# Four instead of seven buffers for the scatter rows and weights of the routed tiles (cross attention and a top-2 mixture of experts on one core)

## What is computed

```python
x = x + xattn(layernorm(x), ctx)                 # 16 heads, causal
scores = sigmoid(xf @ gate_w + bias)
top_scores, top_idx = top_k(scores, 2)           # normalised to sum 1
up = einsum('th,ehi->tei', xf, up_w) + up_b
eo = einsum('tei,eih->teh', gelu(up), down_w) + down_b
combined = einsum('teh,te->th', eo * 0.1, w)     # the two chosen experts
shared = (gelu(xf @ sw_up + sb_up) @ sw_down + sb_down) * 0.1
out = shared + combined;  out = out / (max|out| + 1e-6)
x = x + out
```

## Time and profile before

| | us |
|---|---|
| median of three runs | 898.97 |
| the three runs | 898.99, 898.97, 893.63 |
| the profiled execution | 898.99 |
| its span, first to last instruction | 897.3 |
| around the span (898.99 - 897.3) | 1.7 |
| mean granted PE clock of the span, share of 2.4 GHz | 0.963 |
| busy over the span: PE; DVE; ACT; POOL | 810.9 (90%); 650.1 (72%); 652.1 (73%); 556.1 (62%) |

### The profile page before, as it was taken

How to read it: one execution, slowest core, us unless ns; L and a number is a source line. 1 busy time by engine, 2 the same in 40 slices (tenths; PEclk the granted TensorE clock), 3 DMA queues, 4 the chain that set the end, 5 groups by cost and what they waited for, 6 DMA issues and landing times.

```text
span 897.3 us, 21771 instructions
## 1 busy us (share of the span) xinstructions
PE 810.9 (90%) x7005; PEld 549.7 (61%) x7005; DVE 650.1 (72%) x1767; ACT 652.1 (73%) x1185; POOL 556.1 (62%) x647
## 2 busy tenths in 40 slices
PE   3899999989999999999887639999999999999994
PEld 1355555545555555554455527888888888888773
DVE  6665668777677787765664446878787878777797
ACT  3478897877877877876695628988888888889630
POOL 7267565877878787876565733065656565667531
PEclk9999999989999999998898868999999999999998
DMA  4533543441222222211001124576777787891983
GB/s 118 163 119 106 190 138 107 124 153 55 69 68 74 74 59 85 79 47 48 26 23 54 52 72 153 194 265 233 267 235 264 240 284 274 296 291 63 235 241 105
DMA packets 101382, 128.84 MB, mean 144 GB/s; under 512 B 21143, under 2 KB 81367, under 8 KB 95255
## 3 DMA queue, kind: packets, MB, share of 16 engines
q1 hardware_dynamic: 92183, 108.04, 37.9%
q0 software_dynamic: 9088, 19.42, 6.1%
HBM read 78.79 MB, written 40.56 MB: 133 GB/s over the span
## 4 chain that ended last, share of the span: by engine, by line
PE 60%; issue 11%; DVE 10%; ACT 9%; POOL 8%; another core or an unknown queue 1%; SPq 0%; DMA 0%; ACTq 0%; DVEq 0%; POOLq 0%
PE bank L1291 8%; PE bank L1276 6%; ACT prob L734 5%; POOL y_scratch L1157 5%; PE bank L1373 4%; PE bank L1371 4%; PE bank L1382 4%; PE bank L1384 4%; PE bank L1383 4%; PE bank L1372 4%; PE bank L1296 3%; PE bank L1308 3%; PE bank L1269 3%; PE bank L1251 2%; PE bank L1256 2%
## 5 line engine op out<-in xcount | busy, mean ns | idle before, releaser
L734 ACT ACTIVATE prob<-bank,padb,sc 120x512 f32<-120x512 f32 x256 | 178.3, 777 | 80.0 <-PE bank L1296 72.0
L1157 POOL DMA_INDIRECT y_scratch<-yo,ti x156 | 156.7, 1004 | 123.3 <-DVE yo L1067 86.8
L1135 POOL TENSOR_SCALAR_AFFINE_SELECT prob<-prob 120x512 f32<-120x512 f32 x256 | 162.3, 637 | 86.7 <-ACT prob L734 81.5
L804 DVE TENSOR_REDUCE nm<-bank 128x4 f32<-128x480 f32 x256 | 150.4, 650 | 68.2 <-PE bank L1276 68.2
L1046 DVE TENSOR_TENSOR gl<-gf,gh 128x512 fp32r<-128x512 f32 x220 | 153.3, 699 | 56.0 <-ACT gh L780 49.5
L1150 POOL DMA_INDIRECT xs_scratch<-x2r,idx x128 | 126.9, 992 | 49.6 <-issue 32.9
L780 ACT ACTIVATE gh<-gf 128x512 fp32r<-128x512 f32 x220 | 138.5, 629 | 5.1
L1291 PE MATMUL bank<-qblk,kT 32*120 32x512 f32 x512 | 116.3, 652 | 0.1
L775 ACT ACTIVATE gf<-bank,wt 128x512 f32<-128x512 f32 x156 | 105.9, 679 | 0.2
L775 ACT ACTIVATE gf<-bank,shb 128x512 f32<-128x512 f32 x64 | 43.6, 682 | 49.4 <-remote 17.6
L1276 PE MATMUL bank<-kblk,qT 32*128 32x480 f32 x512 | 72.5, 633 | 0.0
(11 more groups left out here) (194 smaller groups left out, 1663.5 us busy)
## 6 DMA issues: line engine op xcount, KB each, us to landing
wt<-w_scratch SPq DMA_DIRECT2D x39, 1032.0 KB
xt<-xs_scratch SPq DMA_DIRECT2D x39, 280.0 KB
w_scratch<-x2t SPq DMA_DIRECT2D x8, 1024.0 KB, 5.2
wt<-y_scratch SPq DMA_DIRECT2D x28, 256.0 KB, 5.0
xs_scratch<-padc SPq DMA_DIRECT2D x15, 280.0 KB, 3.8
x<-in_x SPq DMA_DIRECT2D x16, 256.0 KB, 3.1
qblk<-qT SPq DMA_DIRECT2D x64, 64.0 KB
x_scratch<-x SPq DMA_DIRECT2D x16, 256.0 KB, 2.5
```

The lines of the kernel that those rows point to most:

```text
L734: e.activation(prob[u % NP][0:LK, :], banks[bi][0:LK, :], ACT.Exp, scale=sc[0:LK, 0:1], bias=padb[0:LK, t:t + 1]).then_inc(a_ex, 1)
L804: e.tensor_reduce(nm[:, g, i // 2, :], bk[:, 0:480].rearrange("p (j k) -> p j k", j=4), AX.X, ALU.max, negate=True).then_inc(v_mx, 1)
L1135: e.affine_select(out=pv, in_=pv, compare_op=ALU.is_ge, fill=0.0, base=0, pattern=[[0, 4], [1, 128]], channel_multiplier=-1).then_inc(p_cu ...
L1157: e.indirect_dma_start(y_dram, bass.IndirectOffsetOnAxis(ap=ti_[r % NWS][:, c:c + 1], axis=0), yo_[r % NYO][:, c, :], None).then_inc(d_y[r ...
```

## The change

NWS goes from 7 to 4. So there are four pairs `ws`, `ti` in place of seven, and the wait in `t_w` is for `yo` and `send` of tile r-4 in place of r-7, from r = 4 in place of r = 7. Nothing else is touched; tensors allocated later in SBUF can lie up to 96 bytes lower in each partition (three buffers of 16 bytes of `ws` and three of `ti`).

```diff
-NX, NP, RG, NWT, NXT, NWS, NYO, NF, NFX = 5, 8, 5, 4, 3, 7, 3, 10, 15
+NX, NP, RG, NWT, NXT, NWS, NYO, NF, NFX = 5, 8, 5, 4, 3, 4, 3, 10, 15
```

## The result

| | before | four pairs |
|---|---|---|
| median of 21 runs each, us | 895.04 (892.71 to 903.11) | 903.25 (900.24 to 910.39) |
| ratio to before, 95% interval | | 1.0083 (1.0064 to 1.0102) |
| profiled execution, its span, us | 898.99, 897.3 | 905.56, 903.8 |

The changed kernel is 0.8% slower, some 7.4 us (0.0083 x 895). The forecast, no change, is wrong by that much; the ratio lies within 1% of before, as the largest chance had it, but 1.0083 x 898.99 = 906.5 us, on the scale of the profiled execution, is past the end of the range (903.0) and 0.9 us above rival 1's full price of 905.6. Only the runs of both kernels that stood beside each other compare: of the kernel before itself the median of 21 is 4 us under the median of the first three.

A forecast was written before the change was run, and what follows sets the result against it. PE was taken to bound the routed tiles, with the new DVE waits covered before reaching it: 898.99 + 0 = 898.99, forecast 899.0 us. The range was 893.2 to 903.0 us.

The forecast's parts named there:

- the largest chance: Whole kernel's time: within 1% of before, given 0.95; faster by over 1% had 0.01, slower by over 1% 0.04.
- rival 1: Routed tiles: late sends' waits pass undiluted to PE, at worst all 6.6 us, 905.6 us; chance 0.06.
- What bounds, the period, the new wait, its order: Routed tiles: PE bounds, 6.45 us a tile; `t_w` of r now waits for the send of r-4.
- the half on `yo`: Wait in `t_w`: `yo` of r-4 is one whole tile back in DVE's order, so waiting for it costs nothing.
- Spare time and landing: Send of r-4 to index write: 1.63 us spare from POOL's release, landing taken as 1.27 us, 0.36 left.
- Size of the waits: `t_w` on DVE: late landings in 12 of 35 tiles, by 0.0 to 1.7 us, together 6.6 us.
- Who waits, and the cover: Work behind DVE's wait: largest wait 1.7 us under smallest cover 2.18, DVE regains up to 1.32 a tile; PE cost 0.
- the banks: Way through `gelu` to PE: 0.27 us of cover, then 1.91 until PE needs the bank, 2.18 in all.
- Rival 2: Reuse of `ti` closes a loop that sets the pace from a 2.95 us landing; at 4.0 us, 917 us; chance 0.03.
- Rival 3: Whole run: median falls on the runs' other level, 893.6 us, a 0.6% gain not from the change; chance 0.10.
- Rival 4: `t_w` on DVE: late landings always covered, no new wait, 899.0 us; chance 0.79 together with the forecast.
- Its reading from the end: Skill page's landing counted from the issue's end: 0.5 us wait in each of 35 tiles, some 18 us of DVE time.

The follow-up runs named there:

- e1: Five pairs `ws`, `ti` in place of the seven of the kernel before; ratio to before 1.0009 (0.9977 to 1.0040).
- e2: Kernel before with its seven pairs and addresses, but `t_w` waits for `yo` and send of r-4; ratio to before 1.0105 (1.0059 to 1.0152).
- e7: Three pairs `ws`, `ti` in place of the seven of the kernel before; ratio to before 1.2492 (1.2424 to 1.2561).
- e4: Changed kernel (four pairs) with three `gf` buffers in place of two; ratio to the kernel before 1.0055 (1.0032 to 1.0078).
- e3: Changed kernel (four pairs) with `t_w` moved later, behind `xl`; ratio to the kernel before 1.0110 (1.0061 to 1.0159).
- e8: Changed kernel (four pairs) with `t_w` one tile later, kept between `yo` and `xl`; ratio to the kernel before 0.9986 (0.9945 to 1.0027).

## Why the prediction was right or wrong

- **What bounds, the period, the new wait, its order:** right. DVE waits for the send of r-4 only, in 9 tiles by the profile's list (12 forecast), and by under 0.1 us or not at all in the other 26; the half on `yo` costs nothing; three more tiles with satisfied waits cost nothing (r = 4 to 6 have no idle time); addresses cost nothing (e1, e2).
- **Spare time and landing:** right in the undisturbed tile. 1.63 us stood, and the landing as DVE sees it is 1.39 us (e7), where 1.27 was taken from SP and 1.42 was the other measured end; 0.24 us were left.
- **Size of the waits:** too small, 6.6 us against 9.9. I had added 0.35 us from a send's last packet to the release, from one undisturbed landing. DVE sees it 0.48 after that packet at the least disturbed (e7), and in the 11 waits of the changed kernel 0.54 to 1.22: the last packet of send r = 14 ends at 677.08 and `ti` starts at 678.26, 1.18 us later.
- **Who waits, and the cover: the step that failed.** "The largest wait expected, 1.7 us, is under the smallest cover, 2.18 [...] Cost on PE: 0." The way to `gelu` was found (of its 0.27 us some 0.17 were cover, 0.10 being the step from `lo` to a `gelu` that waits for it, as from 679.03 + 0.68 to 679.81), and the list then went on to the banks and to `down` only. It left out what comes next in DVE's own order behind the late `lo`: `ye`, which PE's `yT` takes with nothing to spare at its weight load. The smallest cover is 0.31 us, a seventh of what I took. The same step held that "DVE regains up to 1.32 us a tile": it didn't, since 0.95 of that idle time is DVE waiting for ACT, and ACT had been stopped by the same stall (with a third `gf`, e4, it did).
- **The rivals.** Rival 1 is what happened, at its full price but with a condition that I had wrong: not the crowded end alone, each late landing counts, whole but for 0.31 us. Against it I had set the idle time of DVE. Rival 2's loop is not it (most tiles have no wait, the period stays 6.45); at three pairs it exists. Rival 3: no. The medians of 21 runs differ, and both kernels spread by some 10 us. Rival 4: no, the wait shows.
- **The page of the Trainium skill** "DMA: Bandwidth & Descriptors" ("Anatomy of one DMA — SWDGE (gpsimd) path"), read from the start of the issue, gave an estimate of 2.15 us; the trace of e7 has 710.56 - 708.21 = 2.35 us. Its reading from the end, a wait in every tile, is not what any trace with four pairs shows.

## What to carry to other kernels

When an instruction can stall, follow every engine that it feeds to the next thing that the bounding engine needs, through that engine's own order too; the cover is the smallest slack on the shortest of these ways, and an idle gap only helps if its releaser isn't stopped by the same stall. A buffer whose reuse waits for a DMA needs the spare time of its worst landing, not of its usual one: here 0.24 us over the usual cost 0.8%, one more buffer gave 6.45 us and cost nothing, one fewer cost 25%. A short operation that fills another's wait can't be moved a few instructions for free (e3, 1.1%), and moving it into the same hole a tile later can (e8).

## What was not expected of the hardware

- The last of the 32 packets of a 64 KB indirect DMA, one of 4 bytes, ended 1.0 to 1.4 us later than the other 31 when a 16 KB packet of the "instruction" queue ran beside it, in these three cases 0.01 us after the end of that packet (677.07 and 677.08, 614.93 and 614.94, 628.89 and 628.90).
- From such a packet to DVE's `ti` it took 1.18 us, where it is 0.48 us after an undisturbed send (e7).
- With three pairs PE idles a third of the time and the granted clock of the stretch falls to 0.81, and most periods are 0.46 us longer than those whose last 8 us run at 2.4 GHz (12.67 against 12.21).
